# A four-stage fused transformer pair on one core: second layer's softmax sums by way of DRAM, maxima by pick products, biases on GpSimd, partial end passes

## The reference

```python
x = x + tanh(g_xattn[0]) * L0_xattn(ctx, layernorm(x))   # 16 heads of 16, softmax over the keys
x = x + tanh(g_ffn[0])   * L0_ffn(layernorm(x))          # silu(x Wg) * (x Wu), then Wd; 768 hidden, int weights
x = x + tanh(g_xattn[1]) * L1_xattn(layernorm(x), ctx)   # 16 query heads, ONE key/value head of 16
x = x + tanh(g_ffn[1])   * L1_ffn(layernorm(x))          # x (W + low-rank)^T + b
# L0: q, k, v, out all have biases; L1 attention has none
# L1: q = x Wq; k, v = split(ctx Wkv)
# sim = q k^T * 16**-0.5; att = softmax(sim over 120 keys); y = att v; y Wo
```

## Time and profile before

| | us |
|---|---|
| median of 3 runs (lowest, highest) | 2859.21 (2858.59, 2860.34) |
| the profiled execution | 2858.52 |
| its span, first to last instruction | 2856.7 |
| granted TensorE clock over the span | 1.0 |

### The profile page before, as it was taken

How to read it: one execution, slowest core, us unless ns; L and a number is a source line. 1 busy time by engine, 2 the same in 40 slices (tenths; PEclk the granted TensorE clock), 3 DMA queues, 4 the chain that set the end, 5 groups by cost and what they waited for, 6 DMA issues and landing times.

```text
span 2856.7 us, 78111 instructions
## 1 busy us (share of the span) xinstructions
PE 2756.7 (97%) x31776; PEld 2379.1 (83%) x31776; DVE 2596.9 (91%) x4523; ACT 1625.9 (57%) x3161; POOL 1507.7 (53%) x1634
## 2 busy tenths in 40 slices
PE   3999999999999999999999999999999999999999
PEld 3888888888888888888888888888888888888888
DVE  6999999999999999999999999999999999999998
ACT  3555555555555555555555555555555555555555
POOL 3545545654554564455455455545545654554564
PEclk9999999999999999999999999999999999999999
DMA  2000000000000100000000000001000010000000
GB/s 73 29 20 30 24 23 27 24 30 20 30 24 20 30 24 26 24 26 28 20 30 24 24 26 26 28 20 30 24 20 30 24 30 20 29 25 20 30 24 24
DMA packets 78058, 76.09 MB, mean 27 GB/s; under 512 B 7195, under 2 KB 77153, under 8 KB 78050
## 3 DMA queue, kind: packets, MB, share of 16 engines
q1 hardware_dynamic: 78050, 75.99, 8.8%
HBM read 57.30 MB, written 17.56 MB: 26 GB/s over the span
## 4 chain that ended last, share of the span: by engine, by line
DVE 33%; PE 33%; POOL 18%; issue 8%; DMA 3%; SPq 3%; ACT 2%; POOLq 0%; DVEq 0%
PE work L761 8%; POOL zt L327 7%; PE work L762 6%; PE work L763 6%; POOL h_lo L324 6%; PE work L883 5%; DVE m L625 5%; DVE y1f L637 4%; PE scores L853 4%; DVE x L640 4%; POOL zt L331 3%; DVE e L634 3%; DMA x_ln<-xp 3%; SPq L270 2%; POOL zt L334 2%
## 5 line engine op out<-in xcount | busy, mean ns | idle before, releaser
L433 ACT ACTIVATE e<-scores 120x1024 f32<-120x1024 f32 x536 | 528.0, 1024 | 176.3 <-PE scores L863 157.6
L324 POOL TENSOR_TENSOR h_lo<-h_f,h_hi 128x256 fp32r<-128x256 f32 x402 | 430.5, 1078 | 195.3 <-ACT h_hi L392 187.0
L761 PE MATMUL work<-xt_hi_B,w_hi 128*128 128x256 f32 x1608 | 466.2, 290 | 11.3 <-DVE e L573 11.3
L763 PE MATMUL work<-xt_hi_B,w_lo 128*128 128x256 f32 x1608 | 454.3, 283 | 0.0
L762 PE MATMUL work<-xt_lo_B,w_hi 128*128 128x256 f32 x1608 | 454.1, 282 | 0.0
L634 DVE TENSOR_TENSOR e<-e,rz 120x2048 f32<-120x2048 f32 x134 | 405.2, 3024 | 2.3
L327 POOL TENSOR_TENSOR zt<-e 120x512 f32<-120x512 f32 x268 | 341.7, 1286 | 61.4 <-ACT e L433 56.2
L621 DVE TENSOR_REDUCE m<-scores 120x128 fp32r<-120x2048 f32 x134 | 307.1, 2292 | 28.6 <-PE scores L853 21.6
L761 PEld LDWEIGHTS work<-xt_hi_B,w_hi 128*128 128x128 f32 x1608 | 304.9, 190 | 23.0 <-issue 12.0
L762 PEld LDWEIGHTS work<-xt_lo_B,w_hi 128*128 128x128 f32 x1608 | 303.6, 189 | 2.8
L318 POOL TENSOR_TENSOR rstd_B<-var_eps_B,minus_half 128x2 f32<-128x2 f32 x67 | 71.1, 1061 | 443.4 <-DVE var_eps_B L588 443.4
(11 more groups left out here) (200 smaller groups left out, 7612.7 us busy)
## 6 DMA issues: line engine op xcount, KB each, us to landing
x_ln<-xp SPq DMA_DIRECT2D x67, 256.0 KB, 2.7
x_res<-xp SPq DMA_DIRECT2D x67, 256.0 KB, 2.7
y<-y_out SPq DMA_DIRECT2D x67, 256.0 KB, 2.2
ctx_f_A<-cp SPq DMA_DIRECT2D x67, 128.0 KB, 2.5
ctx_f_C<-cp SPq DMA_DIRECT2D x67, 128.0 KB, 2.0
qm<-mT SPq DMA_DIRECT2D x268, 4.0 KB
e<-wi SPq DMA_DIRECT2D x3, 768.0 KB, 5.9
e<-wf SPq DMA_DIRECT2D x2, 512.0 KB, 3.6
```

Source lines behind the costliest of these rows:

```text
L324: return pool.tensor_tensor(h_lo[:, m, :], h_f[:, m % 2, :], h_hi[:, m, :].bitcast(F32), ALU.subtract)
L433: return act.activation(e[0:SC, c, 2 * h:2 * h + 2, :, :].rearrange("p a b n -> p (a b n)"), scores[0:SC, 2 * h:2 * h + 2, :].rearrange("p ...
L761: pe.matmul(out, a_hi, b_hi_, start=first, stop=False, skip_group_check=parts)
L763: last = pe.matmul(out, a_lo, b_hi_, start=False, stop=end, skip_group_check=parts)
```

## The change

- **Second layer's values and ones in one block.** `v1_one` (120 x 32) holds the 16 value columns and 16 ones. `attended1(bank, cc)` is eight matmuls instead of two times eight: each 32-row block of the bank is one head, 16 rows values and 16 rows sum. ACT copies both banks to `yz` (`attended1_out`, 128 x 1024 in all).
- **Packed by way of DRAM, seven DMAs on SP.** `store_yz` (512 KB); `load_z` (one sum per head and query as 128 x 32, 16 KB); `pack` (two, 128 KB each, values to `y1f`); DVE inverts the 128 x 32; `store_rz` (16 KB); `spread_rz` (two, 128 KB each, each row read 16 times, to `rz1`). Then DVE multiplies. The store waits for `yz1`, the loads for the store, `store_rz` for `rz1`, `spread_rz` for that store, all on SP. In DVE's queue the inversion stands between `keys1_odd` and `transposed_lo("A")`, the multiplication behind the moments of B, with y_lo of C, key_max(0), x3, T_lo_B and key_max(1) after it.
- **Maxima by pick products.** `scores1` takes `kz1` and `qt["C"]` directly, and eight fp32r matmuls with `pick` (minus a row selector) and `mT` take the maximum off. `qm1`, `km1` and the four DMAs are gone.
- **Biases on GpSimd.** `add_row` adds wo0's bias to x_res and f1's to a copy of x3 (128 x 512 each); four bias matmuls are gone.
- **Partial end passes.** `one_pass(t)` is written out three times before and three times after a loop of 61; `live(t, n)` leaves out the stages that have no sequence, with one tiny `skipped` instruction for each semaphore. Stage A is live in passes 1 to 64, B one pass later, `down` and C two, second softmax and D three.
- **Order.** PE: scores1(0); down 0 to 3; scores1(1); attended1(0); down 4, 5; attended1(1); attended0; keys_values1; transposes A; keys0; woA; transposes C; queries A; queries C; values0; key_scores(0); woC; transposes B; key_scores(1); gate_up 0; scores0(0); gate_up 1, 2; subtract_max(0); transposes D; gate_up 3; maxima; scores0(1); f1; gate_up 4; subtract_max(1); gate_up 5. GpSimd has both add_heads(1, ...) ahead of hidden_lo(3). `x2_before` is copied earlier; keys are 120 wide instead of 128.
- **Setup.** The first two weight loads are issued ahead of the constants; round r is scaled before w_lo of round r-1 is made; memsets of the padding and of PSUM are gone, as are the bias rows' DMAs.

```diff
-STAGES_BEHIND = 3
-FRONT_X, FRONT_C = 0, 1
+STAGES_BEHIND = 0
+DEPTH = 3
...
+            def store_yz():
+                return sp.dma_start(yz_dram[:, :], yz[:, :, :, :].rearrange("p h c n -> p (h c n)"))
+
+            def pack(to, row, name):
+                rows = yz_dram[:, :].rearrange("(r w d) (h x) -> w h r d x", w=2, d=HD, h=2)
+                for half in range(2):
+                    sp.dma_start(to[64 * half:64 * half + 64, :, :].rearrange("p c n -> p (c n)"), rows[row][half])\
+                        .then_inc(s[name], 16)
+
+            def load_z():
+                return sp.dma_start(z1c[:, :], yz_dram[HD:P:32, :].rearrange("r (k n) -> r k n", n=P // 4))
+
+            def store_rz():
+                return sp.dma_start(rz_dram[:, :].rearrange("r (k n) -> (r k) n", n=P // 4), rz1c[:, :])
+
+            def spread_rz():
+                for half in range(2):
+                    row = rz_dram[:, half * KC * S:(half + 1) * KC * S].unsqueeze(1)
+                    sp.dma_start(rz1[64 * half:64 * half + 64, :, :].rearrange("p c n -> p (c n)"),
+                                 row.to_broadcast([RG, HD, KC * S])).then_inc(s["rz1_spread"], 16)
...
+            def one_pass(t):
+
+                if live(t, 0):
+                    load_ctx("A", t)
...
+                sp.wait_ge(s["yz1"], t)
+                if live(t, 3):
+                    store_yz().then_inc(s["yz_stored"], 16)
...
+                sp.wait_ge(s["yz_stored"], 16 * t)
+                if live(t, 3):
+                    load_z().then_inc(s["z1_loaded"], 16)
...
+                    pack(y1f, 0, "y1_packed")
...
+                sp.wait_ge(s["rz1"], t)
+                if live(t, 3):
+                    store_rz().then_inc(s["rz1_stored"], 16)
...
+                sp.wait_ge(s["rz1_stored"], 16 * t)
+                if live(t, 3):
+                    spread_rz()
...
+            for t in range(FIRST, FIRST + DEPTH):
+                one_pass(t)
+            with nc.sync.Fori(FIRST + DEPTH, FIRST + iterations) as t:
+                one_pass(t)
+            for t in range(FIRST + iterations, last_t + 1):
+                one_pass(t)
...
+            def add_row(to, x, row):
+                return pool.tensor_tensor(to[:, :, :], x[:, :, :], bias_rows[:, row:row + 1, :].to_broadcast([P, NT, D]), ALU.add)
...
+                pool.wait_ge(s["A1_exp"], nth(0, 2, t - 1))
+                if live(t, 1):
+                    add_heads(1, 0)
+                pool.wait_ge(s["A1_exp"], nth(1, 2, t - 1))
+                if live(t, 1):
+                    add_heads(1, 1).then_inc(s["A1_zb"], 1)
+                else:
+                    skipped().then_inc(s["A1_zb"], 1)
                 pool.wait_ge(s["G_hi"], nth(0, 6, t))
-                hidden_lo(3).then_inc(s["G_lo"], 1)
-                add_heads(1, 1).then_inc(s["A1_zb"], 1)
+                if live(t, 2):
+                    hidden_lo(3).then_inc(s["G_lo"], 1)
...
+                pool.wait_ge(s["ld_x_res"], 16 * (t - 1))
+                if live(t, 1):
+                    add_row(x_res, x_res, 0).then_inc(s["x_res_biased"], 1)
...
+                pool.wait_ge(s["res_C"], t)
+                if live(t, 3):
+                    add_row(x3_biased, x3, 1)
...
+            def attended1_out(bank, cc):
+                return act.activation(yz[:, :, cc, :], two(bank, 2), ACT.Copy)
...
             def query_out(st, bank):
                 if st == "C":
-                    act.activation(qm1[:, 0, :], bank[:, :], ACT.Copy)
-                    return act.activation(qm1[:, 1, :], bank[:, :], ACT.Copy)
+                    return act.activation(qt[st][:, :], bank[:, :], ACT.Copy)
...
+                dve.wait_ge(s["z1_loaded"], 16 * t)
+                if live(t, 3):
+                    dve.reciprocal(rz1c[:, :], z1c[:, :]).then_inc(s["rz1"], 1)
+                else:
+                    skipped().then_inc(s["rz1"], 1)
+                dve.wait_ge(s["T_hi_A"], t)
+                if live(t, 0):
+                    transposed_lo("A", W[1]).then_inc(s["T_lo_A"], 1)
...
+                dve.wait_ge(s["rz1_spread"], 32 * t)
+                dve.wait_ge(s["y1_packed"], 32 * t)
+                if live(t, 3):
+                    dve.tensor_tensor(y1f[:, :, :], y1f[:, :, :], rz1[:, :, :], ALU.mult).then_inc(s["yC"], 1)
...
-                        last = pe.matmul(scores[:, r, odd * S:(odd + 1) * S], km1[g, odd, :],
-                                         qm1[g, odd, cc * S:(cc + 1) * S], start=odd == 0, stop=True, skip_group_check=True)
+                        pe.matmul(scores[:, r, odd * S:(odd + 1) * S], kz1[g, odd, :], qt["C"][g, cc * S:(cc + 1) * S],
+                                  start=odd == 0, stop=False, skip_group_check=True)
+                for odd in range(2):
+                    for r in range(RG):
+                        g = slice(32 * r, 32 * r + 32)
+                        last = pe.matmul(scores[:, r, odd * S:(odd + 1) * S], pick[g, 2 * cc + odd, :], mT[g, :],
+                                         start=False, stop=True, skip_group_check=True)
                 return last
...
-            def attended1(bank, v, cc):
-                return per_head(bank, lambda g, par: v[0:SC, 32 * par:32 * par + 32], cc,
-                                lambda r, par: e1[0:SC, cc, r, par, :], 0, S)
...
+            def attended1(bank, cc):
+
+                for r in range(RG):
+                    for odd in range(2):
+                        half, block = divmod(2 * r + odd, RG)
+                        last = pe.matmul(bank[32 * block:32 * block + 32, half * S:(half + 1) * S], v1_one[0:SC, :],
+                                         e1[0:SC, cc, r, odd, :], start=True, stop=True)
+                return last
```

More of the change, by code:

```diff
@@ L337, in heads_total, with skipped @@
                 return pool.tensor_tensor(z0[0:SC, c, :], zt[0:SC, c, 0, :], zt[0:SC, c, 1, :], ALU.add)
-            with nc.gpsimd.Fori(FIRST, last_t + 1) as t:
-                pool.wait_ge(s["G_hi"], nth(5, 6, t - 1))
-                hidden_lo(2).then_inc(s["G_lo"], 1)
-                pool.wait_ge(s["A1_exp"], nth(0, 2, t))
-                add_heads(1, 0)
+            at = itertools.count()
+            def skipped():
+                n = next(at)
+                return pool.memset(spare["pool"][:, n:n + 1], 0.0)
@@ L372, in _ @@
+            with nc.gpsimd.Fori(FIRST + DEPTH, FIRST + iterations) as t:
+                one_pass(t)
+            for t in range(FIRST + iterations, last_t + 1):
+                one_pass(t)
         @block.scalar
@@ L378, in _, with round_hi @@
                 .then_inc(s["cst_r"], 1)
[L379 to L382 removed]
+            def round_hi(r):
+                name, n = ROUNDS[r]
                 act.wait_ge(s["w_scaled"], r + 1)
@@ L685, in _ @@
-                residual(x1, x_res, W[0]).then_inc(s["res_A"], 1)
-                dve.wait_ge(s["res_A"], t)
-                moments("B", x1, t).then_inc(s["ln_eps_B"], 1)
+                if live(t, 1):
+                    low(y_lo["A"][:, :, :], two(W[3], KC), y_hi["A"][:, :, :])
+                dve.wait_ge(s["v1_pad"], t)
+                if live(t, 2):
+                    keys1_odd(W[2]).then_inc(s["kz1_odd"], 1)
+                else:
+                    skipped().then_inc(s["kz1_odd"], 1)
@@ L911, in _ @@
+                pe.wait_ge(s["T0_exp"], nth(1, 2, t))
+                if live(t, 3):
+                    scores1(1).then_inc(s["T1_mm"], 1)
+                else:
+                    skipped(scores[:, 0, :]).then_inc(s["T1_mm"], 1)
+                pe.wait_ge(s["G_h"], nth(1, 6, t))
+                if live(t, 3):
+                    attended1(W[3], 0).then_inc(s["yz0_mm"], 1)
+                else:
+                    skipped(W[3]).then_inc(s["yz0_mm"], 1)
                 pe.wait_ge(s["G_lo"], nth(1, 6, t))
-                down(W[2], 3).then_inc(s["dn_mm"], 1)
@@ L977 @@
+                pe.wait_ge(s["res_D"], t)
+                if live(t, 1):
+                    gate_up(W[0], 5).then_inc(s["G_mm"], 1)
+                else:
+                    skipped(W[0]).then_inc(s["G_mm"], 1)
+            for t in range(FIRST, FIRST + DEPTH):
+                one_pass(t)
+            with nc.tensor.Fori(FIRST + DEPTH, FIRST + iterations) as t:
+                one_pass(t)
+            for t in range(FIRST + iterations, last_t + 1):
+                one_pass(t)
 def kernel(**inputs):
```

966 lines of the change are left out of this document (670 added, 296 removed), and 9 rows, old and new, of the table per_pass.

## The result

The changed kernel takes 3287.4 us (median of 4 runs, 3282.1 to 3291.8), the kernel before 2859.4 on the same chip: 1.150 times the time, 95% interval 1.148 to 1.152. Forecast were 2833, with a range that ended at 2918. The profiled execution took 3282.1, its span is 3280.1.

What follows compares the result with a forecast made beforehand. TensorE's own queue was taken to set the time, 41.84 us a pass before; 50.4 (start) + 61 x 42.1 (whole passes) + 213 (partial passes) = 2831.6 us of span, 2833.4 beside the median; range 2770 to 2918.

Steps and rivals of the forecast that it cites:

- TensorE's work: TensorE's work in a pass: falls from 40.4 us to 38.8 (38.6 in the walk, bounds 38.4 to 40).
- Down 3 waits 0.65 for GpSimd: TensorE's down 3 starts 0.65 us late, since h_lo 3 stands behind add_heads(1,1) on GpSimd, which meets normalise(0).
- Setup and ends: Loop starts at 50.4 us; six partial passes sum to 213 instead of 251; under 195 or over 235 would be wrong.
- Rival 4: Partial end passes cost as much as whole ones through latency and instruction fetch: +38 us, 2871; chance 0.08.
- Store of yz 3.0: Second layer's round trip, first DMA leg: storing 512 KB takes 3.0 us, bounds 2.2 and 3.6.
- Load of the sums 1.75: Round trip, second DMA leg: loading 16 KB in 128 B pieces takes 1.75 us, bounds 1.4 and 2.4.
- Store of the inverses 1.7: Round trip, third DMA leg: storing 16 KB in 128 B pieces takes 1.7 us, bounds 1.4 and 2.4.
- Spread 2.5: Round trip, last DMA leg: 2.0 us as ctx_C, second transfer issued 0.5 later, 2.5 in all; bounds 2.3 and 3.2.
- 28.6 + 13.5 = 42.1: Walk through one pass: sums landed at 28.6 us, then 13.5 through spread, multiply and maxima to scores0; 42.1 a pass.
- rival 2: Each of four DMA legs 0.3 us longer, VectorE stuck at their head: +1.1 a pass, 2901; decides from 9.4; chance 0.22.
- Rival 3: GpSimd and VectorE block each other fully; normalise(0) waits for the whole add_heads: 42.8 us a pass, 2876; chance 0.08.
- Rival 1: The round trip is shorter or hidden: 41.4 us a pass, 2790; chance 0.16.

Runs made afterwards that it cites:

- e1: Changed kernel without the store of the inverses and their spread, so layer 2's attention is not divided by its softmax sums (constant factor 1); 2855.6 us.
- e8: e1 with hidden_lo(3) moved ahead of add_heads(1, 1) on GpSimd; 2852.4 us.
- e17: Changed kernel without load of sums, store of inverses or spread; VectorE inverts and multiplies constants, values packed by eight direct transfers; 2798.3 us.
- e3: Changed kernel with the pack issued behind the spread instead of ahead of store_rz; 3352.3 us.
- e5: Changed kernel with 36 unread filler matmuls of 256 columns on TensorE ahead of its wait for yC_lo; 3161.9 us.
- e12: Changed kernel without the store of yz: sums go SBUF to SBUF in two transfers, values in eight, spread of 8 rows; 2891.7 us, 1.012 times the kernel before.
- the hybrid: e10 with hidden_lo(3) ahead of add_heads(1, 1) on GpSimd; 2953.2 us.
- e13: e12 with the inverses stored twice, so that the spread's DRAM side has 16 rows outermost; 2919.0 us, 1.020 times the kernel before.
- e10: Changed kernel with sums loaded SBUF to SBUF in two transfers, store_rz ahead of the pack, spread and pack one 8-row transfer each; 2950.5 us.
- e6: Changed kernel with spread and pack each one transfer of 8 rows outermost, order kept; 3090.1 us.
- e2: Changed kernel with the spread as one transfer of 8 rows instead of two of 4, DRAM layouts half by half; 3210.6 us.
- e14: e12 with key_max(0) before VectorE's multiply, and transposes B, key_scores(1) and gate_up 0 ahead of woC on TensorE; 2987.7 us, 1.045 times the kernel before.

## Why the prediction was wrong, step by step

- **TensorE's work**: right. scores1 with its eight picks, in e1, takes 0.78 + 0.53 (1513.18, 1513.96 and 1514.49 below) where 1.08 + 0.4 was assumed; attended1 is 0.89 where 0.88 was. VectorE is busy 34.78 us of e1's pass, where 35 was.

```profile
1513.18 1.15 PE L1236 MATMUL scores<-qt_C,kz 32*128 32x256 f32 x16
1513.96 0.60 PE L1241 MATMUL scores<-mT,pick 32*128 32x256 f32 x8
1514.49 0.39 PE L1133 MATMUL work<-w_hi,h_hi 128*128 128x256 f32 x1
...
1517.60 0.39 PE L1133 MATMUL work<-w_hi,h_hi 128*128 128x256 f32 x1 [0.69 <-POOL h_lo L375]
...
1522.82 1.07 PE L1276 MATMUL work<-e,v_one 120*32 120x256 f32 x16
1523.71 1.49 PE L1261 MATMUL work<-e,v_pad 120*32 120x128 f32 x48
```

- **Down 3 waits 0.65 for GpSimd**: it waits, 0.69 here. That an order without this wait would be worth something was not claimed, and e8 shows that it is not.
- **Setup and ends**: start 50.95 for 50.4; first three passes 103.9 for 102. The last three took 133.9 for 111, but 113.7 in e17, which has no trip: the 20 us go with three trips and their clock. The sum of 238 is over the forecast's sign of 235, but six whole passes of 49.04 would be 294. Rival 4 is out.
- **Store of yz 3.0**: 2.7. **Load of the sums 1.75**: 2.2.
- **Store of the inverses 1.7**: the first step that failed. By itself it is 1.43 (e3), so the row-based price was even high; in its place it was 3.4. I had set the pack aside as two transfers that nobody waits for soon, and did not ask what stands behind them in the queue.
- **Spread 2.5**: the second, and the larger: 5.4. I took ctx_C's 2.0 for 128 KB as the price of 128 KB. ctx_C has 128 partitions outermost, the spread has 4 rows; both of its transfers share the same four engines, so that the second adds all its data and not 0.5 (and the load of ctx_C, set aside as having slack, runs among them). The nearest row was nearest in bytes and not in shape, and the bounds (2.3 to 3.2) had the same flaw.
- **28.6 + 13.5 = 42.1**: the structure holds. From the multiply round to the next store of yz the walk has 42.1 - 9.45 = 32.65; e5 and e12, at or near the full clock, show 33.0 and 33.1. Ten runs of this order of TensorE and VectorE (the hybrid with e8's order on GpSimd is the tenth), with trips from 9.7 to 15.15, keep to pass = trip + 33 + up to 2 for the clock.
- **The clock**: missing from the working. The forecast had TensorE waiting 0.5 here and there, where no row of before shows a clock under 1.00. What it costs grows with the wait before woC. With 1.45 us in the mean, by the rows of its products (e12), the clock fell in 3 of the 51 passes between 300 and 2500 us, with 1.7 (e13) in 16 of 51, with 1.9 (e10) in 27 of 50, with 2.6 (e6) in 39 of 48, with 4.0 and 5.1 (e2, changed kernel) in every one, and the rest went from 33.1 to 34.9. The sum: 42.1 + 4.7 (trip) + 0.4 (rest) + 1.9 (clock) = 49.1; measured 49.0. A usual pass of e12, its wait and its windows:

```profile
1465.07 0.39 PE L1136 MATMUL work<-w_hi,y_hi_C 128*128 128x256 f32 x1 [1.49 <-DVE y_lo_C L848]
...
1449.00:1491.80 42.80, 39.56 (x462) 34.53 (x454) 34.85 (x67) 23.42 (x46) 24.45 (x27) 1.00 0.12 38
```

- **Rivals**: rival 2 named the mechanism and the point (9.4, VectorE stuck at the head) and missed the size: +0.3 a leg where two legs had +1.7 and +2.9; the four legs, 8.95 in the forecast, came to 13.7. Rival 3 is out with e17's 41.45. Rival 1 is what e17 measured by leaving the trip out: 2798 where 2790 stood.

## What to carry to other kernels

A transfer's price is its shape and its place in the queue before it is its bytes: count the outermost dimension on both sides, and list what was issued ahead of it and is not yet over. A long wait on TensorE can cost twice, once by its length and once by the clock behind it: 5.5 us of waiting brought 1.9 more a pass. One piece of 1.45 (e12) mostly did not, while 0.5 and 1.1 close together (e14) did in nearly every pass, so a wait's length alone does not tell, and the clock has to be read in the rows. And before work is moved to make room for a late operand, look at what that work was hiding.
